# Router logits of two mixture-of-experts stages: from one block behind the transposes to one row tile at a time between them

## What is computed

```python
flat = layernorm(x)                      # 625 x 768
# first feed-forward layer
logits = flat @ router_w.T               # 8 experts
top_w, top_i = top_k(softmax(logits), 2)
for e in range(8):
    h = gelu(flat @ w1[e] + b1[e])       # 768 -> 192
    out += w_e * (h @ w2[e] + b2[e])     # 192 -> 768
# second feed-forward layer
logits = x @ router_w.T                  # 8 experts
tok_unit = normalize(x @ probe_w.T)      # 24 probes
logits += bias(mean(x), tok_unit, router_emb, energy, fatigue)
g, idx = top_k(logits, 2)
# relu(.)**2 experts, gates softmax(g)
```

## Time and profile before

| | us |
|---|---|
| median of 3 runs | 1539.88 |
| lowest, highest | 1535.57, 1540.15 |
| the profiled execution | 1541.18 |
| its span | 1538.6 |
| PE busy in the span | 1242.8 |
| DVE busy | 885.8 |
| ACT busy | 726.5 |
| POOL busy | 646.8 |
| first feed-forward stage, from its first instruction to the last product of its slots | 492 to 650 |
| second feed-forward stage | 1366 to 1538.6 |

### The profile page before, as it was taken

The page is one execution under the profiler, slowest core; times in us unless marked ns, Lnnn a source line. Parts: engine busy times, 40 slices in busy tenths (PEclk is TensorE's granted clock), DMA queues, the critical chain, the costliest instruction groups (busy, mean ns, idle before and its releaser), DMA issues. The chain is left out here.

```text
span 1538.6 us, 32053 instructions
## 1 busy us (share of the span) xinstructions
PE 1242.8 (81%) x9846; PEld 934.0 (61%) x9847; DVE 885.8 (58%) x1710; ACT 726.5 (47%) x1089; POOL 646.8 (42%) x625
## 2 busy tenths in 40 slices
PE   8999584793847488818899999999999967863996
PEld 6776474783734477617566666666666645543874
DVE  8961658696557734344666666566656527664000
ACT  8995410783232455423445645454554524120663
POOL 0067655783700223223355555555555540002243
PEclk9999585796868589958999999999999987875998
DMA  3000210001023587576689998899999886645443
GB/s 132 1 1 4 83 17 1 1 0 63 21 72 104 153 301 270 179 219 245 191 264 266 284 279 273 239 283 292 277 297 272 249 223 183 186 98 172 86 98 52
DMA packets 115419, 247.39 MB, mean 161 GB/s; under 512 B 23566, under 2 KB 53515, under 8 KB 115345
## 3 DMA queue, kind: packets, MB, share of 16 engines
q1 hardware_dynamic: 80241, 162.83, 31.3%
q0 software_dynamic: 35104, 83.58, 23.1%
HBM read 217.06 MB, written 58.36 MB: 179 GB/s over the span
## 5 line engine op out<-in xcount | busy, mean ns | idle before, releaser
L627 PE MATMUL r_pO<-ring,r_rowsT 128*128 x2520 | 422.3, 327 | 0.0
L627 PEld LDWEIGHTS r_pO<-ring,r_rowsT 128*128 128x128 f16 x2520 | 244.2, 98 | 154.7 <-issue 1.3
L1865 DVE SCALAR_TENSOR_TENSOR ring<-q_wstage,ring 128x768 f16<-128x768 f32 x198 | 175.0, 952 | 55.9 <-ACT ring L1824 54.6
L1805 POOL DMA_INDIRECT acc_dram<-r_msg,r_scol x70 | 131.6, 1881 | 155.3 <-PE r_pT L1926 100.5
L1824 ACT ACTIVATE ring<-q_wstage 128x768 f16<-128x768 f32 x198 | 148.8, 830 | 26.5 <-issue 26.5
L1853 ACT ACTIVATE r_msg<-r_pO,slot_inv 128x768 f32<-128x768 f32 x70 | 62.8, 897 | 191.1 <-PE r_pO L627 191.0
L477 POOL DMA_INDIRECT slot_inv<-qinv_dram,slot_pair x112 | 125.8, 1123 | 57.4 <-issue 33.5
L432 POOL DMA_INDIRECT slot_dram<-table_record,table_rowi x80 | 101.1, 1264 | 104.7 <-issue 104.0
L395 PE MATMUL acc<-oh_d,oh_s 125*125 125x512 f16 (+1 forms) x800 | 137.3, 311 | 0.0
L1926 PE MATMUL r_pT<-r_S,q_parts 128*128 128x128 f16 x852 | 100.4, 221 | 8.6 <-DVE r_S L1882 5.7
L1872 DVE TENSOR_TENSOR r_rowsT<-r_pT,r_rowsT 128x512 f16<-128x512 f32 x71 | 48.7, 686 | 101.4 <-ACT r_rowsT L1833 101.3
(11 more groups left out here) (404 smaller groups left out, 2379.5 us busy)
## 6 DMA issues: line engine op xcount, KB each, us to landing
q_wstage<-in_L_gnn_W_rel_dram SPq DMA_DIRECT2D x33, 2304.0 KB, 14.2
stage<-in_L_gnn_W_dram SPq DMA_DIRECT2D x6, 768.0 KB, 7.2
wparts<-in_L_ffn_w_dram SPq DMA_DIRECT2D x8, 576.0 KB, 4.7
f_stage<-in_L_ffn_w_dram SPq DMA_DIRECT2D x8, 576.0 KB, 12.1
f_stage<-in_L_ffn_w_fast_dram SPq DMA_DIRECT2D x8, 576.0 KB, 6.3
f_stage<-in_L_ffn_w_slow_dram SPq DMA_DIRECT2D x8, 576.0 KB, 8.3
f_stage<-in_L_ffn_h_fast_dram SPq DMA_DIRECT2D x8, 576.0 KB, 10.0
down_dram<-f_stage SPq DMA_DIRECT2D x8, 576.0 KB, 4.4
```

The lines of the kernel that those rows point to most:

```text
L627: ins = eng.matmul(out, x, w[:, h * n:(h + 1) * n], start=first and x is xh and w is wh, stop=last and x is xl, **kw)
L1805: eng.indirect_dma_start(out=K.acc_dram[u % 2], out_offset=bass.IndirectOffsetOnAxis(ap=scol[:, u:u + 1], axis=0), in_=msg[:, u, :], in_of ...
L1865: ins_ = eng.scalar_tensor_tensor(wring[:, slot, 1, k, :], wstage[:, slot, k, :], W_SCALE, wring[:, slot, 0, k, :], ALU.mult, ALU.subtract)
```

## The change

Two hooks are added to Transposed: on PE a function runs after the transposes of each tile, on DVE after lo of each tile (ACT had such a hook). The stage uses them so:

- PE transposes the router's weights behind tile 1 instead of ahead of tile 0; ACT rounds them behind hi 2, DVE makes rT lo behind lo 2.
- PE computes the logits of tile i - 2 behind the transposes of tile i, for i = 2, 3, 4, and those of tiles 3 and 4 at the end. Each waits only for the copy of its own tile.
- The logits go to PSUM bank 1 instead of bank 4.

No instruction is added or taken away apart from waits on semaphores.

```diff
--- before.py
+++ after.py
@@ -513,7 +513,7 @@
                 last = eng.copy(out[:, a], src[:, a])
         last.then_inc(self_s[("copied_even", "copied_odd")[i % 2]], 1)
 
-    def vector(self, eng):
+    def vector(self, eng, beside=None):
         K, s = self.K, self.s
         link = chain(eng, K.dve_chain)
         if self.norm:
@@ -544,6 +544,8 @@
                 prepare(i + 1)
             eng.wait_ge(s["hi_ready"], i + 1)
             eng.tensor_tensor(self.parts[:, i, 1, :], self.src[:, i, :], self.parts[:, i, 0, :], ALU.subtract).then_inc(s["lo_ready"], 1)
+            if beside:
+                beside(i)
             if i >= 2 and i % 2 == 0:
                 self._copy(eng, i - 1)
 
@@ -564,7 +566,7 @@
                 self._copy(eng, i - 1)
         self._copy(eng, NT - 1)
 
-    def tensor(self, eng):
+    def tensor(self, eng, beside=None):
         K, s = self.K, self.s
         for i in range(NT):
             eng.wait_ge(s["lo_ready"], i + 1)
@@ -575,6 +577,11 @@
                     last = eng.transpose(self.psum[i % 2][:, a, k * PP:k * PP + P], self.parts[:, i, a, k * 128:(k + 1) * 128],
                                          K.ident16[0:P, 0:P])
             last.then_inc(s["transposed"], 1)
+            if beside:
+                beside(i)
+
+    def wait_tile(self, eng, i):
+        eng.wait_ge(self.s[("copied_even", "copied_odd")[i % 2]], i // 2 + 1)
 
     def wait_done(self, eng):
         eng.wait_ge(self.s["copied_even"], (NT + 1) // 2)
@@ -1290,11 +1297,13 @@
                 eng.scalar_tensor_tensor(w_down[0:FH, 1, e, :, :].rearrange("p t c -> p (t c)"), down_stage[:, e % DOWNS, :], W_SCALE,
                                          w_down[0:FH, 0, e, :, :].rearrange("p t c -> p (t c)"), ALU.mult, ALU.subtract).then_inc(s["cut_lo"], 1)
 
-            T.vector(eng)
-
-            eng.wait_ge(s["rt_hi"], 1)
-            rps = psum[:, 0, 0:KC * NR].rearrange("p (k r) -> p k r", r=NR)
-            eng.scalar_tensor_tensor(rT[:, 1, :, :], rps, W_SCALE, rT[:, 0, :, :], ALU.mult, ALU.subtract).then_inc(s["rt_lo"], 1)
+            def router_lo(i):
+                if i == 2:
+                    eng.wait_ge(s["rt_hi"], 1)
+                    rps = psum[:, 0, 0:KC * NR].rearrange("p (k r) -> p k r", r=NR)
+                    eng.scalar_tensor_tensor(rT[:, 1, :, :], rps, W_SCALE, rT[:, 0, :, :], ALU.mult, ALU.subtract).then_inc(s["rt_lo"], 1)
+
+            T.vector(eng, router_lo)
             eng.wait_ge(s["small_loaded"], 32 - 16 * layer)
             link(eng.tensor_scalar(b2p[:, 0, :], b2[:, :], W_SCALE, None, ALU.mult))
             eng.scalar_tensor_tensor(b2p[:, 1, :], b2[:, :], W_SCALE, b2p[:, 0, :], ALU.mult, ALU.subtract).then_inc(s["b2_ready"], 1)
@@ -1312,7 +1321,7 @@
                 for e in range(EARLY_CUTS):
                     cut_down(e)
             eng.wait_ge(s["logits_ready"], 1)
-            link(eng.tensor_scalar(lg[:, :, :], psum[0:P, 4, 0:NT * NR].rearrange("p (i r) -> p i r", r=NR), 1.0 / W_SCALE, None, ALU.mult))
+            link(eng.tensor_scalar(lg[:, :, :], psum[0:P, 1, 0:NT * NR].rearrange("p (i r) -> p i r", r=NR), 1.0 / W_SCALE, None, ALU.mult))
             eng.wait_ge(s["pool_ready"], pool_ready)
             logit = lg[:, :, 0:EXP]
             if layer == 1:
@@ -1468,10 +1477,13 @@
                     eng.wait_ge(s["scattered"], 16 * (t - YS + 1))
                 eng.activation(y[:, t % YS, :].rearrange("p (b n) -> p b n", b=2), pY[t % 2], ACT.Copy, scale=gate[:, t:t + 1]).then_inc(s["y_ready"], 1)
 
-            T.scalar(eng)
-            eng.wait_ge(s["rt_ready"], 1)
-            rps = psum[:, 0, 0:KC * NR].rearrange("p (k r) -> p k r", r=NR)
-            eng.activation(rT[:, 0, :, :], rps, ACT.Copy, scale=W_SCALE).then_inc(s["rt_hi"], 1)
+            def router_hi(i):
+                if i == 2:
+                    eng.wait_ge(s["rt_ready"], 1)
+                    rps = psum[:, 0, 0:KC * NR].rearrange("p (k r) -> p k r", r=NR)
+                    eng.activation(rT[:, 0, :, :], rps, ACT.Copy, scale=W_SCALE).then_inc(s["rt_hi"], 1)
+
+            T.scalar(eng, router_hi)
             if layer == 0:
                 for e in range(DOWNS):
                     cut_down(e)
@@ -1500,21 +1512,32 @@
 
         @block.tensor
         def _(eng):
-            eng.wait_ge(s["router_loaded"], 16 * (1 + layer))
-            if layer == 1:
-                eng.wait_ge(s["pool_ready"], 1)
-            for k in range(KC):
-                last = eng.transpose(psum[:, 0, k * NR:(k + 1) * NR], rw[:, k * 128:(k + 1) * 128], K.ident[0:NR, 0:NR])
-            last.then_inc(s["rt_ready"], 1)
-            T.tensor(eng)
-            T.wait_done(eng)
-            eng.wait_ge(s["rt_lo"], 1)
-            for i in range(NT):
+            def turn_router():
+                eng.wait_ge(s["router_loaded"], 16 * (1 + layer))
+                if layer == 1:
+                    eng.wait_ge(s["pool_ready"], 1)
+                for k in range(KC):
+                    last = eng.transpose(psum[:, 0, k * NR:(k + 1) * NR], rw[:, k * 128:(k + 1) * 128], K.ident[0:NR, 0:NR])
+                last.then_inc(s["rt_ready"], 1)
+
+            def logits(i):
                 tok_ = slice(i * P, (i + 1) * P)
-                out = psum[0:P, 4, i * NR:(i + 1) * NR]
+                out = psum[0:P, 1, i * NR:(i + 1) * NR]
+                T.wait_tile(eng, i)
                 for k in range(KC):
                     last = three_products(eng, [out], xT[:, 0, k, tok_], xT[:, 1, k, tok_], rT[:, 0, k, :], rT[:, 1, k, :], k == 0, k == KC - 1)
-            last.then_inc(s["logits_ready"], 1)
+                return last
+
+            def between(i):
+                if i == 1:
+                    turn_router()
+                if i == 2:
+                    eng.wait_ge(s["rt_lo"], 1)
+                if i >= 2:
+                    logits(i - 2)
+            T.tensor(eng, between)
+            logits(NT - 2)
+            logits(NT - 1).then_inc(s["logits_ready"], 1)
 
             eng.wait_ge(s["pool_ready"], pool_ready)
             eng.wait_ge(s["members_ready"], 1)
```

## The result

| | before | changed |
|---|---|---|
| median, us | 1536.94 (21 runs) | 1530.89 (21 runs) |
| lowest, highest | 1533.15, 1541.79 | 1528.37, 1536.65 |
| ratio, with its 95% interval | | 0.9961 (0.9950 to 0.9971) |
| profiled execution, its span | 1541.18, 1538.6 | 1528.37, 1526.7 |
| PE, DVE, ACT busy | 1242.8, 885.8, 726.5 | 1235.5, 885.2, 725.9 |

The changed kernel is faster by 6.05 us between the medians, 4.5 to 7.7 by the interval, where 4.25 was forecast.

What follows compares the result with a forecast made beforehand. The second stage's chain of waits through PE's logits was taken to bound the kernel. Gains of 4.15 us there and 0.1 in the first stage, 4.25 together, take the median from 1539.88 to 1535.7 us; range 1531.0 to 1540.0.

Steps and rivals of the forecast that it cites:

- What bounds the kernel: Second stage: an unbroken chain of waits from transposes through logits, routing and first gather to scatters; logits time saved shortens the end.
- the three idle times: PE, second stage, from tile 2's transposes to the products: waits of 0.93, 0.93 and 2.29 us vanish, gaining 4.15 us.
- The cost of the blocks: PE, second stage: 1.95 us per logits tile and 1.44 us per tile's transposes, 12.64 us in place of 16.79.
- The first stage: Logits ready 3.9 us sooner but DVE's four lo cuts, behind ACT's later last copy, hold the take-up: gain 0.1 us.
- The loss of 0.5 us: First stage, the lower bound on its gain: four changes of work on PE at 0.1 us each, priced at nothing.
- What was costed at nothing: Router transposes in PE's wait for lo 2, DVE's b2 and embedding work, the first stage's later cuts: no time added.
- The row store: Second stage, ahead of the first gather: if served in order, through at about 1405, 2 us ahead of need.
- Rival 1: Row store holds the second stage's first gather, leaving 0 to 4.15 us gain; 1537.8 us, up to 1539.8; chance 0.12.
- Rival 2: PE reaches its high clock in the stretch of transposes and products without idle time; 1529 to 1533 us; chance 0.07.
- Rival 3: Both stages gain because DVE's cuts don't hold the first; needs the last copy as early as before; 1532 us; chance 0.02.
- Rival 4: Products run longer between transposes; gain gone at 0.6 us more per logits tile, 1544 us at twice that; chance 0.04.
- "Within 0.3%": Whole time: a change too small to tell from none, bound 4.6 us, forecast 0.4 us inside it; chance 0.56.

Runs made afterwards that it cites:

- twice_first: The changed kernel with the products of tiles 3 and 4 computed twice in the first stage only; 1646.12 us, one run.
- hi_cuts_early: The changed kernel with ACT's first two hi cuts ahead of its last copy in the first stage; 1643.58 us, ratio 0.9941 to the kernel before.
- both_early: hi_cuts_early plus, in both stages, router turned ahead of tile 0 and logits of tile i - 1 behind tile i's transposes; 1644.87 us, ratio 0.9962 to before.
- twice_second: The changed kernel with the products of tiles 3 and 4 computed twice in the second stage only; 1644.09 us, one run.
- again: The changed kernel unchanged, profiled and timed a second time; 1534.55 us, ratio 0.9983 to the kernel before.

## Why the prediction was right and where it failed

**What bounds the kernel, and the three idle times: right.** The chain was the one described; the idle times of the earlier trace rows are gone, and the gain reaches the first gather and the first scatter whole (18.20 and 24.16 us, against 18.18 and 24.24 before).

**The cost of the blocks: the step that failed.** "A logits tile costs 9.76 / 5 = 1.95 us, a tile's transposes 1.44 us" takes PE rows as if they could be laid end to end. A row's length reaches to the end of its last instruction, an end that the profile models, and the next block starts before that. In the changed profile 12 transposes take 1.21 to 1.23 us from start to start (1.44 by their row), 18 products 1.89 (2.05 by their row). From the start of tile 2 to the last product I reckoned 1.44 + 12.64 = 14.08 us; it took 13.33. Three transposes at 0.21 to 0.23 each and 0.09 on the products make these 0.75 us: 4.90 instead of 4.15. The chain of waits shows pieces without overlap, and the sum should have been made from such starts. The Trainium skill (TensorE: Matmul & The Clock Gate, Single matmul latency) gives about 175 ns for the drain of a matmul, at either level of the clock. The overlap here, 0.16 to 0.23 us, agrees, as far as modelled ends can show it.

**The first stage: mechanism right, the same size off.** I let tile 4's transposes end 8.22 us behind T2; they ended at 505.61, 7.64 behind. The last copy, the hi cut and the four lo cuts (6.76 us) followed as described, and the take-up came 0.72 us nearer instead of 0.1. That the cuts bound it is shown by twice_first (no cost) and hi_cuts_early (3.3 us less). The loss of 0.5 us that I set as the other bound doesn't follow from four changes at 0.1 each; they make 0.4.

**What was costed at nothing, and cost nothing:** the router's transposes ran at 1363.38 in PE's wait for lo 2; the work on b2 and the embedding was done at 1375.63, 3.1 us ahead of the take-up; the late cuts of the first stage moved nothing that shows in its 12.23 us from take-up to gather.

**The row store.** I had it through at about 1405 in the time of before. It was issued at 1380.55 there, and with the 25.15 us of both_early it would land at 1405.7. That it goes first and the copy behind it after, which the trace of before could not tell, is shown by both_early, where 1.74 MB of that copy moved only after it. In the changed kernel it was issued at 1370.00 and by the same 25.15 us would land at 1395.2. That is 0.9 us ahead of the token numbers, where I had reckoned 2; and since the gather of both_early started 0.27 us behind the landing, but 0.8 us behind the token numbers elsewhere, the store had 1.5 us until it would have cost anything. A further 1.9 us off the stretch used that up.

**The rivals.** Rival 1 (the store) did not come true, but was an estimated 1.5 us away. Rival 2 (the high clock) is refuted: 0.50 over 13.33 us and over 17.18 in twice_second. The Trainium skill's rule (TensorE: Matmul & The Clock Gate, Part 1) that sustained matmul activity releases the throttle doesn't hold for these two stretches of products. Rival 3 needed the last copy out of the way, which hi_cuts_early did. Rival 4 is refuted: a block takes 2.05 us by its row, and 90 products took 9.67 against 9.76 before.

**The number and the chances.** The forecast was 1535.7, the measurement 1530.89, 0.1 us below the range. Of the 4.8 us between them 2.9 are the baseline: the median of the three runs shown lay that much above the median of the 21. 1.4 are the blocks (5.6 instead of 4.25), the last 0.5 is within the scatter. So the term that put the number off most is the baseline, 1539.88 taken from three runs as if it were exact, which measured 1536.94; the mis-sized blocks alone would have left the time inside the range, at 1534.3. That it came out 0.1 us below the range, and not above its lower end, is chance. The range allowed the sum almost nothing below the forecast except the clock; it should have held the uncertainty of a median of three (its runs spread over 4.6 us) on the low side too. "Within 0.3%" was given 0.56 on a sum 0.4 us from that bound; the mis-sized blocks put it on the other side.

## What to carry to other kernels

Add up PE blocks by the distance from start to start, or by the pieces of the chain of waits; lengths of single rows count the drain of each block once more, here 0.2 us a block. Before interleaving work, follow each stage to the engine that takes its result: the same edit gave 4.9 us where DVE waited for PE and 0.7 where DVE was behind with other work, and there moving two cuts on ACT gave 3.3 more. Where a small change is judged by a profile, compare the stretch from one fixed point to the next, never the spans: here they differed by 11.9 us for an effect of 5.6.

## What the runs showed of the hardware

**A transfer of 125 partitions took a third of the DMA engines' time.** While the store or the seed ran alone the share was 0.32 at 131 GB/s; cut into 112 and 13 partitions it was 1.04 at 398 GB/s. The Trainium skill (DMA: Bandwidth & Descriptors, Why a DMA increments its semaphore by 16 and not by 1) says that a transfer goes to the largest number of engines up to 16 that divides the slowest dimension of both its sides, for 125 that is 5: 5 of 16 are 0.31, the 31.5% of the earlier trace rows. I had read that figure as a rate and not asked why.

**VectorE's and GpSimd's rows trade lengths at the head of the second stage.** The second stage's first transposes start 4.96 us or 4.21 us behind the stage's first issue, whatever the kernel. The two first normalisations on DVE and POOL's work beside them, before and then in the changed kernel:

```profile
1367.74 2.01 DVE L537 TENSOR_SCALAR f_xn<-x,f_mv,f_sd 125x768 f32<-125x768 f32 x2
1367.95 0.52 POOL L1233 MEMSET f_hT<- 97x512 f16 x1
```

```profile
1357.94 1.55 DVE L537 TENSOR_SCALAR f_xn<-x,f_mv,f_sd 125x768 f32<-125x768 f32 x2
1358.15 0.94 POOL L1240 MEMSET f_hT<- 97x512 f16 x1
```

Where POOL's row is short DVE's is long, and the other way round. Of the fourteen profiles eleven have the first form (first normalisation 1.42 or 1.43 us, this MEMSET 0.52) and three the second (0.68 and 0.94): the changed kernel, twice_second and hi_cuts_early, but not again, which is the changed kernel too. The Trainium skill (SBUF — State Buffer, SBUF: two separate sides) says that the two share a pair of ports under an exclusive lock, held for a whole instruction; the rows fit that, but no run here took POOL's work away. This is 0.75 us of the 5.65 by which the second head shrank in the profile, and no part of the change.
